# Four plain copies in a chain of factors written as max(x, x), in a fused recurrent layer on one core

## The reference

```python
xn = _ln(x, ln1_w, ln1_b)
sx = _token_shift(xn, state[:, i1])
xxx = jnp.tanh((xn + sx * maa_x) @ maa_w1).reshape(b, l, 5, 1, EXTRA_MAA)
xxx = jnp.matmul(xxx, maa_w2).reshape(b, l, 5, E)
x5 = xn[:, :, None] + sx[:, :, None] * (maa_stack + xxx)
w = jnp.exp(-jnp.exp(time_decay + jnp.tanh(x5[:, :, 1] @ decay_w1) @ decay_w2))
r, k, v = x5[:, :, 3] @ Wr.T, x5[:, :, 0] @ Wk.T, x5[:, :, 2] @ Wv.T
g = jax.nn.silu(x5[:, :, 4] @ Wg.T)
def step(s, rkvw):
    r_t, k_t, v_t, w_t = rkvw
    a = k_t[:, :, :, None] * v_t[:, :, None, :]
    out = jnp.einsum('bhk,bhkd->bhd', r_t, u * a + s)
    return (a + w_t[:, :, :, None] * s, out)
```

## Time and profile before

| | |
|---|---|
| median of 3 runs | 1547.56 us (1545.41 to 1550.09) |
| profiled execution, first to last instruction | 1549.0 us |
| PE busy | 1505.6 us, 97% |
| DVE busy | 898.2 us, 58% |
| POOL busy | 595.1 us, 38% |
| ACT busy | 516.3 us, 33% |
| the four copies | 20.0 + 11.2 + 5.3 + 19.7 us in 128 instructions |
| granted TensorE clock, mean | 0.995 |

### The profile page before, as it was taken

The page is one execution under the profiler, slowest core; times in us unless marked ns, Lnnn a source line. Parts: engine busy times, 40 slices in busy tenths (PEclk is TensorE's granted clock), DMA queues, the critical chain, the costliest instruction groups (busy, mean ns, idle before and its releaser), DMA issues.

```text
span 1549.0 us, 50439 instructions
## 1 busy us (share of the span) xinstructions
PE 1505.6 (97%) x22156; PEld 1093.0 (71%) x22156; DVE 898.2 (58%) x1990; ACT 516.3 (33%) x910; POOL 595.1 (38%) x528
## 2 busy tenths in 40 slices
PE   8998999999999999999999999999999999999798
PEld 7876866767777676867767677676866767777464
DVE  3658566466665646666465655655666465654542
ACT  1323423333332333423333332333423333342332
POOL 3354425244262533526144261533525244262321
PEclk9999999999999999999999999999999999999999
DMA  7011102011020211102011010201102011020110
GB/s 295 17 44 42 39 8 72 17 39 53 26 61 8 66 26 36 54 6 75 17 39 53 27 54 14 67 26 35 55 5 75 17 39 53 13 62 7 45 42 27
DMA packets 56442, 68.01 MB, mean 44 GB/s; under 512 B 23264, under 2 KB 40032, under 8 KB 55200
## 3 DMA queue, kind: packets, MB, share of 16 engines
q1 hardware_dynamic: 56224, 64.79, 13.6%
HBM read 43.75 MB, written 8.39 MB: 34 GB/s over the span
## 4 chain that ended last, share of the span: by engine, by line
PE 91%; ACT 2%; DVE 2%; issue 2%; SPq 1%; POOL 1%; DMA 0%; ACTq 0%; DVEq 0%; POOLq 0%
PE pair L1195 32%; PE pair L1214 21%; PE at_ps L1124 5%; PE pair L1206 4%; PE at_ps L1117 4%; PE att_ps L1186 3%; PE pair L1222 3%; PE pair L1238 2%; PE pair L1259 2%; PE pair L1300 2%; PE att_ps L1173 2%; PE pair L1302 2%; PE att_ps L1382 1%; DVE x L746 1%; PE pair L1307 1%
## 5 line engine op out<-in xcount | busy, mean ns | idle before, releaser
L1195 PE MATMUL pair<-x,wts 128*128 128x256 f32 x1760 | 402.1, 384 | 0.2 <-POOL x L512 0.2
L1195 PEld LDWEIGHTS pair<-x,wts 128*128 128x128 f32 x1760 | 328.7, 191 | 49.2 <-issue 6.8
L512 POOL TENSOR_TENSOR x<-x,xnT 128x1024 f32<-128x1024 f32 (+1 forms) x79 | 155.8, 1973 | 242.7 <-DVE x L746 242.7
L746 DVE SCALAR_TENSOR_TENSOR x<-pair,vecs,sx 128x256 f32<-128x256 f32 x316 | 130.5, 477 | 189.0 <-PE pair L1238 91.8
L947 ACT ACTIVATE at<-at_ps 128x512 f32<-128x512 f32 x128 | 76.0, 594 | 295.8 <-PE at_ps L1124 258.1
L1195 PE MATMUL pair<-yT,wts 128*128 128x256 f32 x512 | 117.5, 383 | 1.5 <-DVE yT L838 1.5
L1214 PE MATMUL pair<-wts,cen 128*128 128x512 f32 x240 | 114.1, 618 | 2.7 <-DVE x L746 2.5
L1124 PE MATMUL at_ps<-rm,kc 128*16 128x128 f32 (+1 forms) x2048 | 110.5, 275 | 2.9 <-issue 2.9
L1214 PE MATMUL pair<-wts,yT 128*128 128x512 f32 x240 | 111.4, 607 | 0.0
L1214 PE MATMUL pair<-wts,sx 128*128 128x512 f32 x240 | 109.1, 598 | 0.0
L1195 PEld LDWEIGHTS pair<-yT,wts 128*128 128x128 f32 x512 | 94.9, 190 | 16.2 <-DVE gT L782 3.0
(11 more groups left out here) (210 smaller groups left out, 2611.6 us busy)
## 6 DMA issues: line engine op xcount, KB each, us to landing
rm<-rst SPq DMA_DIRECT2D x1024, 12.0 KB, 1.8
xu<-in_x SPq DMA_DIRECT2D x16, 512.0 KB
wts<-in_wts SPq DMA_DIRECT2D x8, 1024.0 KB, 13.7
kvs<-in_s SPq DMA_DIRECT2D x32, 256.0 KB, 3.0
s<-in_s SPq DMA_DIRECT2D x32, 256.0 KB, 3.0
x<-in_x SPq DMA_DIRECT2D x15, 512.0 KB, 4.2
out<-sx SPq DMA_DIRECT2D x15, 512.0 KB, 2.9
prev<-in_prev SPq DMA_DIRECT2D x32, 4.0 KB, 3.9
```

The costliest lines, as they stand in the source:

```text
L512: gp.tensor_tensor(t, t, old, ALU.add).then_inc(x5_ready, 1)
L746: last = ve.scalar_tensor_tensor(seqs(mixed(name, a), g), ps[:, :, g * L:(g + 1) * L], vecs[:, vec, g:g + 1], seqs(sx, g), ALU.add, ALU.mult)
L1195: last = pe.matmul(ps[:, g // 2, TB * (g % 2):TB * (g % 2 + 1)], wts[:, m, k, g * P:(g + 1) * P], source[:, k, :], start=(k == 0), stop=(k ...
```

## The change

Each of the four copies becomes a tensor_tensor operation with the same tile as both inputs and max as its operation. Output, element counts, access patterns, semaphore increments and the place of each instruction in VectorE's order stay. No instruction is added or taken away on any engine, and none moves. The line numbers between the first and the second edit fall by one (L659 becomes L658, and so on up to L675), and from L678 on they are as before.

```diff
-                ve.tensor_copy(
-                               bass.AP(kc4[b], 0, [[G * 8 * REC4, P], [REC4, n4], [12, 3], [1, 4]]),
-                               kn[:, :, 0:3, :]).then_inc(kchain, 1)
+                ve.tensor_tensor(bass.AP(kc4[b], 0, [[G * 8 * REC4, P], [REC4, n4], [12, 3], [1, 4]]),
+                                 kn[:, :, 0:3, :], kn[:, :, 0:3, :], ALU.max).then_inc(kchain, 1)
...
-                ve.tensor_copy(bass.AP(kc16[b], 0, [[G * 2 * REC16, P], [REC16, n16], [48, 3], [1, 16]]),
-                               kc[:, :, 0:48].rearrange("p n (l t) -> p n l t", t=16)).then_inc(kchain, 1)
+                near = kc[:, :, 0:48].rearrange("p n (l t) -> p n l t", t=16)
+                ve.tensor_tensor(bass.AP(kc16[b], 0, [[G * 2 * REC16, P], [REC16, n16], [48, 3], [1, 16]]),
+                                 near, near, ALU.max).then_inc(kchain, 1)
...
-                ve.tensor_copy(du[:, :, 1], cuc[:, :, 0]).then_inc(kchain, 1)
+                ve.tensor_tensor(du[:, :, 1], cuc[:, :, 0], cuc[:, :, 0], ALU.max).then_inc(kchain, 1)
...
-                ve.tensor_copy(kt[:, :, 48:64], kb[:, :, 48:64]).then_inc(kchain, 1)
+                ve.tensor_tensor(kt[:, :, 48:64], kb[:, :, 48:64], kb[:, :, 48:64], ALU.max).then_inc(kchain, 1)
```

## The result

| | before | changed |
|---|---|---|
| median of 15 runs each, side by side | 1549.39 us (1545.3 to 1555.74) | 1554.07 us (1551.71 to 1556.94) |
| ratio | | 1.0031, 95% interval 1.0019 to 1.0042 |
| profiled execution's span | 1549.0 us | 1551.8 us |
| VectorE busy | 898.2 us | 910.5 us |

The change makes the kernel slower by 4.7 us (interval 2.9 to 6.5). The forecast was 1548.4 us with a range up to 1553.0, and a chance of 0.10 for a slower kernel: wrong.

A forecast was written before the change was run, and what follows sets the result against it. TensorE, busy 92.04 of 92.60 us in a regular step, was taken as the bound. Thirteen steps' 0.65 us plus 0.2 in the last gave 0.85 on a median of 1547.56: 1548.4 us, range 1544.5 to 1553.0.

The forecast's parts named there:

- What bounds it, and the prices: TensorE bounds regular steps; on VectorE the edits cost 0.20 + 0.20 + 0 + 0.03 = 0.43 us a chain.
- The first sequence's chain: Sixteen chains ahead of 5.40 us of VectorE idle time: the added 0.43 us fits, cost 0.
- Gate one: L656 delays L810, then ScalarE's L938, then TensorE's mixKR; 0.22 us taken as room, mixKR moving 0 to 0.05 us.
- sign for wrong covers: A regular step of over 92.95 us would prove the assumed covers wrong; 92.6 to 92.7 us was expected.
- kt1, z and the covers behind: Second sequence's chain: kt1 has 0.99 us of room; z comes 0.17 late, covered by 0.27 idle before L1206, cost 0 to 0.03.
- The last step: L656 costs nothing there; L678, on the path behind L810 to the kernel's end, passes on its 0.20 us: cost 0.2.
- The sum: Thirteen regular steps at 0.05 us, 0.65, plus 0.2 at the end: 0.85 us in all, giving 1548.4 us.
- A turn lost to GpSimd: Second sequence's chain: L656 runs behind GpSimd's L555, about 0.4 us later; 6.3 us slower, 1553.9 us; chance 0.07.
- Freed of GpSimd: L656 and L699 no longer wait for GpSimd, second chain ends 0.3 us sooner: 2 us gained, 1545.6 us; chance 0.08.
- Everything exposed: TensorE waits for each of the 32 chains, so all 13.8 us show: 1561 us; chance 0.02.
- The form costs nothing: On VectorE, max of the same tile twice runs at the copy's rate: 1547.6 us; chance 0.05.

The follow-up runs named there:

- first-sequences kernel: Two-operand forms only in the first sequence's (b = 0) chains, copies for the second, against the kernel before: ratio 1.0011, step 92.58 us.
- gn_var ahead: Changed kernel with VectorE's L810 moved ahead of the chain part holding L656: 1.0008 of before, step 92.58 us; with copies kept 0.9994.
- The first copy alone: Kernel before with only L656 in the two-operand form, the other three left as copies: ratio 1.0024, step 92.77 us.
- the memset alone: Kernel before, all copies kept, with a 192-element memset in its own tile just ahead of L810: ratio 1.0010, step 92.73 us.
- the two delays together: Kernel before with L656 in the two-operand form and a 192-element memset ahead of L810: ratio 1.0024, step 92.91 us.
- the reorderings that open the gate: Changed kernel with L810 ahead of L656, 1.0008 of before; or v before gn_std on ScalarE and gn_rec behind mixK on VectorE, 1.0010.
- v ahead: Changed kernel with ScalarE's eviction of v (L938) moved ahead of gn_std: 1.0031 of before, step 92.76 us.
- the repeat: The changed kernel measured again beside the kernel before, with granted clocks: 1555.78 against 1550.05 us, ratio 1.0036.

## Why the prediction was wrong

**What bounds it, and the prices.** Right: 0.42 us a chain against 0.43 forecast, VectorE's busy time up by 12.3 us against "some 14". The base was low: the forecast started from 1547.56 us, a median of three, and fifteen runs gave 1549.39. That is 1.8 of the 5.7 us between 1548.4 and 1554.07, and no fault of the mechanism.

**The first sequence's chain, cost 0.** Right for the regular step, by the first-sequences kernel; its total of 1.0011 can't be told from no change.

**Gate one.** This is the step that failed: "The distance is 0.22 us, so L938 would end at 447.71, within 0.02 us of the old start ... mixKR moves by 0 to 0.05 us." I took the distance between L938's end and L1238's load for room, because L1206's load follows its own releaser by 0.04 us. The distance is 0.22 or 0.23 us in the kernel before, the changed one, and the one with gn_var ahead, where L938 starts at different causes and idle times. It is 0.22 or 0.23 us in nearly every step of all 14 profiles. It is that load's fixed follow-up time. In the program it stands behind four waits (two for mixK's tile, one for v's, one for h), L1206's behind two; whether their number makes the difference was not tried. mixKR moved by the full delay of L656: 0.19 us a step instead of 0.05, 13 x 0.19 = 2.5 us instead of 0.65. The first copy alone, the memset alone, the two delays together and the reorderings that open the gate show it. The prediction's own sign for wrong covers, a step of over 92.95 us, could not catch this: 92.77 lies above its 92.6 to 92.7 and below that mark.

**kt1, z and the covers behind.** The room at kt1 was right (0.76 us are left). z was not late against mixKR in the changed kernel (forecast: 0.1 to 0.2 us), since mixKR moved back by L656's 0.19 us itself. Where it was late, 0.34 us cost 0.18 (v ahead) and 0.11 cost nothing (gn_var ahead): the cover of some 0.16 was there. Up to 0.23 us behind gate one cost nothing.

**The last step, 0.2.** Its chain behaves as said: VectorE idles for 7.37 us ahead of L810, and L678 stands on the path behind it.

```profile
1463.98 1.22 DVE L810 TENSOR_REDUCE gsum<-yT 128x64 f32<-128x1024 f32 x1 [7.37 <-ACT yT L1026]
...
1465.19 0.55 DVE L678 TENSOR_TENSOR kc<-kT 128x384 f32<-128x384 f32 x1
...
1466.19 1.56 POOL L493 TENSOR_TENSOR rst<-rT,du 128x256 f32<-128x256 f32 x2 [1.60 <-DVE du L684]
```

L493 starts 2.21 us after L810 where it was 2.02: 0.19 us. That it reaches the end was argued from the chain and not tried by itself.

**The sum.** 2.5 + 0.2 = 2.7 us of the 4.7 (2.9 to 6.5) measured. With 2.7 us in place of 0.85 the forecast would have been 1550.3 us, and 1552.1 from the base of fifteen runs. The other 2.0 us had no term in the prediction, and their cause is open. The eighth step's 2.3 us, seen in both profiles of the changed kernel and not in that of before, would be large enough, but the totals above do not bear it out. Of the repeat's 5.7 us, 2.7 are these terms and 1.1 to 1.4 go with the clock; 1.6 to 1.9 us stay open, within what its interval (3.3 to 7.9) allows.

**The rivals.** A turn lost to GpSimd: no, the turns stayed; that its 6.3 us lay near the measured time was chance. Freed of GpSimd: no. L675, L676 before, still shows up to 0.80 us for 8 elements, and L699 kept its wait; of the two pages cited, the trace agrees with "SBUF — State Buffer" of the Trainium skill, Who interferes with whom. Everything exposed: no, some 2.5 us of 13.8. The form costs nothing: no.

## What to carry to other kernels

The time between a releaser's end and the start of what it releases is not room; find it from a second place where the same instruction is released, or from its idle time, and treat an instruction that starts right after its releaser as having none. Where an engine is busy for 99% and its order is fixed, look for every semaphore that its short waits hang on, and ask which instruction of the lengthened engine stands ahead of each: one of four edits carried the whole price of a step here, because it stood ahead of a reduction that another engine waited for. A reordering can open one gate and shut the next (v ahead of gn_std did, through a table load), so measure the step and not only the wait.

## What the runs showed of the hardware

- A copy of 384 fp32 elements took 349 ns and max of the tile with itself 548; at 8 elements both took 163 or 164 ns.
- The 0.19 us on VectorE, ahead of gate one, came out on TensorE at 0.19 us a step; 0.23 us behind it came out at 0. Of two memsets put there, 0.13 us got through, since a copy that waited behind GpSimd took 0.41 us instead of 0.62.
- From the end of L938 to the start of L1238's load it was 0.22 to 0.23 us, whatever had released L938; from the end of L966 to L1206's load 0.04 to 0.05 us.
- TensorE stood idle inside one item for 1.3 to 2.2 us at the same pair of matmuls in all 14 profiles, and started again 1.2 to 1.5 us after a packet of the queue of kind instruction had landed. In seven of the 14 it was then granted 1.2 GHz for 3.4 us. With the fall the step took 96.0 to 96.7 us, without it 93.8 to 94.9. At another place 1.56 us of idle were followed by a fall in one profile, and 2.12 us by none in another.
